# Attention kernel for 32 images: one lane's softmax rows normalised before the turn, its values product taken on two tiles at once

## What is computed

```
# layer 0
h    = group_norm(x) * gn_w + gn_b                     # 32 groups of 4 channels
q,k,v = split(qkv_w @ h + qkv_b)                        # 128 channels each
attn = softmax(q^T k * C**-0.5)                         # 1024 x 1024 per image
x    = x + proj_w @ (v @ attn^T) + proj_b
# layer 1
q,k  = Wq @ x + bq, Wk @ x + bk                         # 16 channels each
v    = Wv @ x + bv                                      # 128 channels
attn = softmax(q^T k)
out  = gamma * (v @ attn^T) + x
```

## Time and profile before

| | |
|---|---|
| median of 3 runs | 1571.02 us (1569.89 to 1573.38) |
| the profiled execution | 1575.76 us |
| its span, first to last instruction | 1573.7 us |
| transposing DMAs | 512, two in a slot |
| slots with tiles | 257 |

### The profile page before, as it was taken

How to read it: one execution, slowest core, us unless ns; L and a number is a source line. 1 busy time by engine, 2 the same in 40 slices (tenths; PEclk the granted TensorE clock), 3 DMA queues, 4 the chain that set the end, 5 groups by cost and what they waited for, 6 DMA issues and landing times.

```text
span 1573.7 us, 43918 instructions
## 1 busy us (share of the span) xinstructions
PE 1482.2 (94%) x16777; PEld 1116.9 (71%) x16777; DVE 1285.6 (82%) x2508; ACT 1218.2 (77%) x1698; POOL 1240.4 (79%) x1027
## 2 busy tenths in 40 slices
PE   4899999999999999999899999999999999999977
PEld 2577777776777777777677777677777777777766
DVE  5678888888888888888788888888888878888885
ACT  3578878887877887878788887887878878888774
POOL 3788888888878887878788888788788878888653
PEclk9899999999999999999999999999999999999999
DMA  3799999999999999999999999999999999999999
GB/s 76 135 161 199 203 197 204 198 206 204 198 195 194 207 203 203 202 193 209 189 202 211 202 194 202 196 202 203 195 199 210 203 190 204 203 193 199 192 200 181
DMA packets 1081437, 305.21 MB, mean 194 GB/s; under 512 B 1068272, under 2 KB 1068944, under 8 KB 1081232
## 3 DMA queue, kind: packets, MB, share of 16 engines
q1 hardware_dynamic: 1066688, 270.42, 105.4%
q10 hardware_dynamic: 14544, 31.99, 6.0%
HBM read 17.13 MB, written 16.78 MB: 22 GB/s over the span
## 4 chain that ended last, share of the span: by engine, by line
SPq 66%; PE 17%; issue 5%; DVE 4%; DMA 3%; ACT 2%; POOL 1%; DVEq 0%; POOLq 0%; ACTq 0%
SPq L299 66%; DMA pt<-rows 3%; PE mixed L823 3%; PE mixed L825 3%; PE mixed L824 3%; PE scores L778 2%; DVE nmax L572 2%; PE scores L779 1%; PE scores L780 1%; DVE rows L589 1%; PE scores L808 1%; PE bank_w L889 1%; PE bank_w L897 1%; ACT scores L457 1%; POOL rows L358 1%
## 5 line engine op out<-in xcount | busy, mean ns | idle before, releaser
L823 PE MATMUL mixed<-v_head,pt 128*128 128x129 f16 x4096 | 719.5, 222 | 35.7 <-DMA pt<-rows 34.6
L572 DVE TENSOR_REDUCE nmax<-scores 128x1 f32<-128x1024 f32 x512 | 620.5, 1217 | 154.8 <-PE scores L808 141.8
L825 PE MATMUL mixed<-v_head,pt 128*128 128x129 f16 x4096 | 718.7, 220 | 0.0
L824 PE MATMUL mixed<-v_tail,pt 128*128 128x128 f16 x4096 | 718.7, 219 | 0.0
L358 POOL TENSOR_TENSOR rows<-prob,rows 128x1024 f16<-128x1024 f32 x256 | 545.4, 2130 | 21.3
L353 POOL TENSOR_SCALAR rows<-prob 128x1024 f16<-128x1024 f32 x256 | 267.9, 1046 | 233.4 <-ACT prob L452 229.9
L457 ACT ACTIVATE scores<-scores,nmax 128x1024 f32<-128x1024 f32 x256 | 278.7, 1089 | 204.2 <-DVE nmax L572 204.2
L823 PEld LDWEIGHTS mixed<-v_head,pt 128*128 128x128 f16 x4096 | 399.0, 97 | 47.1 <-DMA pt<-rows 45.6
L824 PEld LDWEIGHTS mixed<-v_tail,pt 128*128 128x128 f16 x4096 | 405.7, 99 | 2.3
L825 PEld LDWEIGHTS mixed<-v_head,pt 128*128 128x128 f16 x4096 | 397.0, 97 | 0.0
L589 DVE SCALAR_TENSOR_TENSOR rows<-scores,rows 128x1024 f16<-128x1024 f32 x256 | 313.0, 1222 | 35.6 <-ACT rows L465 35.4
(11 more groups left out here) (110 smaller groups left out, 1852.8 us busy)
## 6 DMA issues: line engine op xcount, KB each, us to landing
out_dram<-y ACTq DMA_DIRECT2D x64, 256.0 KB, 3.8
x_raw<-in_x_dram ACTq DMA_DIRECT2D x29, 512.0 KB, 5.2
pt<-rows SPq DMA_TRANSPOSE x512, 5.4
x_raw<-in_x_dram SPq DMA_DIRECT2D x3, 512.0 KB, 4.4
w_qkv<-in_L_conv_qkv_w_dram SPq DMA_DIRECT2D x3, 64.0 KB, 4.1
b_qk<-in_L_conv_bk_dram SPq DMA_DIRECT2D x8, 0.1 KB, 2.3
b_qk<-in_L_conv_bq_dram SPq DMA_DIRECT2D x8, 0.1 KB, 1.9
w_proj<-in_L_conv_proj_w_dram SPq DMA_DIRECT2D x1, 64.0 KB, 4.8
```

The source lines that it names most:

```text
L572: nc.vector.reduce_max(nmax[l][:, tile.i % TILES:tile.i % TILES + 1], scores[l][:, :], AX.X, negate=True).then_inc(maxed[l], 1)
L823: mm(mixed[l][:, 0:C + 1], head, vh[:, p, m, 0:C + 1], start=(m == 0), stop=False)
L824: mm(mixed[l][:, 0:C], head, vt[:, p, m, :], start=False, stop=False)
L825: done = mm(mixed[l][:, 0:C + 1], tail, vh[:, p, m, 0:C + 1], start=False, stop=(m == TILES - 1))
```

## The change

1. Lane 1's rows are normalised when they are split. `exponent1` also sums the row (`accum_out=row_sum`). A second, 1-column activation scales the sum by 1/4096 (`sum_down`). VectorE inverts it (`invert1`), and head and tail are multiplied with the inverse in place of the constant 4096. `head_row1` now waits for `inverted[1]`.
2. Lane 1's values product is `attend_pair`. It takes two tiles (the even one and the odd one behind it) at once, with v as the stationary operand and 2 x 128 columns of `pt` as the moving one. It runs in the slot of the odd tile + 3, so in every second slot. The result has channels in partitions, so `norm` and `back` are gone for lane 1, and one addition of 256 columns for the pair (`add_pair`) follows in the same slot. Lane 1's ring of `pt` has 6 buffers, since a pair frees two at once.
3. VectorE's order is now: both row maxima, the bias, `invert1`, lane 0's addition, the projection's tail, `tail_row1`, `invert0`, the pair's addition.
4. In the fill, the statistics and the group norm of image 2 stand some slots earlier, and the load of image 2 is issued ahead of 16 small loads.

```diff
-RING = 4
+RING = (4, 6)
...
+KEY_HALVES = (ATTEND, ATTEND)
...
+def pair_at(slot):
+    tile = TILE_AT[1].get(slot)
+    return (LANES[1][tile.i - 1], tile) if tile and tile.i % 2 else None
...
-STATS = Steps(-12, -11, first={1: (-11, -11), 2: (-9, -9)})
-GN = Steps(-10, -9, first={2: (-8, -7)})
+STATS = Steps(-12, -11, first={1: (-11, -11), 2: (-11, -11)})
+GN = Steps(-10, -9)
...
             def exponent1(tile):
                 act.wait_ge(maxed[1], tile.i + 1)
-                nc.scalar.activation(scores[1][:, :], scores[1][:, :], ACT.Exp,
-                                     bias=nmax[1][:, tile.i % TILES:tile.i % TILES + 1],
-                                     scale=1.0).then_inc(exped[1], 1)
+                nc.scalar.activation(scores[1][:, :], scores[1][:, :], ACT.Exp, bias=nmax[1][:, at], scale=1.0,
+                                     accum_out=row_sum[:, at]).then_inc(exped[1], 1)
+                act.wait_ge(exped[1], tile.i + 1)
+                nc.scalar.activation(sum_down[:, at], row_sum[:, at], ACT.Copy,
+                                     scale=1.0 / P_UP).then_inc(summed_down, 1)
...
             def head_row1(tile):
-                act.wait_ge(exped[1], tile.i + 1)
+                act.wait_ge(inverted[1], tile.i + 1)
                 nc.scalar.activation(rows[1][:, tile.i % ROWS, 0, :], scores[1][:, :], ACT.Copy,
-                                     scale=P_UP).then_inc(row_headed[1], 1)
+                                     scale=rinv[1][:, tile.i % TILES:tile.i % TILES + 1]).then_inc(row_headed[1], 1)
...
+            def invert1(tile):
+                dve.wait_ge(summed_down, tile.i + 1)
+                nc.vector.reciprocal(rinv[1][:, at], sum_down[:, at]).then_inc(inverted[1], 1)
...
+            def add_pair(pair):
+                out_free(tile)
+                dve.wait_ge(attended[1], pair[1].i // 2 + 1)
+                nc.vector.scalar_tensor_tensor(out=of_pair(into, pair),
+                                               in0=mixed[1][:, 0:2 * C].rearrange("p (t c) -> p t c", c=C),
+                                               scalar=1.0 / P_UP, in1=of_pair(residual[:, tile.p, :], pair),
+                                               op0=ALU.mult, op1=ALU.add).then_inc(done, 2)
...
+            def attend_pair(pair, half):
+                if half == 0:
+                    for tile in pair:
+                        pe.wait_ge(swung[1][tile.i % RING[1]], swings(tile))
+                    if first.i:
+                        last = LANES[1][first.i - 1]
+                        pe.wait_ge((x1_done, y_done)[last.layer], ADDED[1, last.i])
+                into = mixed[1][:, 0:2 * C].rearrange("p (t n) -> p t n", n=C)
+                for m in range(half * PER_HALF, (half + 1) * PER_HALF):
+                    done = split_product(into, vh[:, p, m, 0:C], vt[:, p, m, :], pt[1][:, r:r + 2, m, :],
+                                         pt[1][:, r:r + 2, TILES + m, :], start=(m == 0), stop=(m == TILES - 1))
...
             def body(slot):
-                here = [lane.get(slot - ATTEND) for lane in TILE_AT]
-                for tile in here:
-                    if tile:
-                        attend(tile)
+                here = TILE_AT[0].get(slot - ATTEND)
+                if here:
+                    attend0(here)
+                for half, offset in enumerate(KEY_HALVES):
+                    if pair := pair_at(slot - offset):
+                        attend_pair(pair, half)
```

More of the change, by code:

```diff
@@ L83, with single_adds, pair_adds, adds_in_order @@
 TILE_AT = [{tile.slot: tile for tile in tiles} for tiles in LANES]
+def pair_at(slot):
+    tile = TILE_AT[1].get(slot)
+    return (LANES[1][tile.i - 1], tile) if tile and tile.i % 2 else None
+def single_adds(slot):
+    return [tile for tile in (TILE_AT[0].get(slot - ADD),) if tile]
+def pair_adds(slot):
+    return [pair for pair in (pair_at(slot - KEY_HALVES[1]),) if pair]
+def adds_in_order():
+    count, added = [0, 0], {}
+    for slot in range(FIRST_SLOT, LAST_SLOT + 1):
+        for tiles in [(tile,) for tile in single_adds(slot)] + pair_adds(slot):
+            count[tiles[0].layer] += len(tiles)
+            added.update({(tile.lane, tile.i): count[tile.layer] for tile in tiles})
+    return added
+ADDED = adds_in_order()
 class Steps:
@@ L271, in swings, with of_pair @@
         def swings(tile):
-            return 16 * (tile.i // RING + 1)
+            return 16 * (tile.i // RING[tile.lane] + 1)
+        def of_pair(image, pair):
+            first, step = pair[0].t, pair[1].t - pair[0].t
+            tiles = image.rearrange("p (t c) -> p t c", c=C)
+            first %= tiles.shape[1]
+            return tiles[:, first:first + step + 1:step, :]
         def qk_bank(im, j):
@@ L530, in body @@
                     qk1_copy(im, h)
-                for lane in range(2):
-                    if tile := TILE_AT[lane].get(slot - ATTEND):
-                        norm(tile)
+                if tile := TILE_AT[0].get(slot - ATTEND):
+                    norm(tile)
                 for im, part in W.at(slot):
@@ L732, in body @@
                     row_max(tile)
+                if tile := TILE_AT[0].get(slot):
+                    row_max(tile)
+                    exp_bias(tile)
+                if tile := TILE_AT[1].get(slot):
+                    invert1(tile)
+                for tile in single_adds(slot):
+                    add_turned(tile)
                 for im, part in W.at(slot - 1):
@@ L739, in body @@
                         v1_tail_out(im, part - V1[0])
[L740 to L744, removed]
-                    dve.wait_ge(turned[tile.lane], tile.i + 1)
-                for tile in added:
-                    (x1_out, y_out)[tile.layer](tile)
                 if tile := TILE_AT[1].get(slot):
                     tail_row1(tile)
-                for lane in TILE_AT:
-                    if tile := lane.get(slot - ATTEND):
-                        invert(tile)
+                if tile := TILE_AT[0].get(slot - ATTEND):
+                    invert0(tile)
+                for pair in pair_adds(slot):
+                    add_pair(pair)
                 for im, h in STATS.at(slot):
@@ L829, in adds_done @@
             def adds_done(slot):
-                for lane in TILE_AT:
-                    if tile := lane.get(slot - ADD):
-                        pe.wait_ge((x1_done, y_done)[tile.layer], tile.n * TILES + tile.t + 1)
+                for tile in single_adds(slot):
+                    pe.wait_ge((x1_done, y_done)[tile.layer], ADDED[0, tile.i])
             def evicted_here(slot):
```

122 lines of the change are left out of this document (63 added, 59 removed).

## The result

The changed kernel takes **1790.08 us** (4 runs, 1787.31 to 1795.71) against 1570.64 before: 1.140 times as long, 95% interval 1.136 to 1.143. The forecast was 1690, with a range of 1630 to 1745. The sign and the pattern were right, the size was not: +219 where +119 was forecast.

What follows compares the result with a forecast made beforehand. SyncE's transposes were taken as the bound, 47.3 us an image, TensorE nearly level. Odd slots 27.2 plus even 24.0 made 51.2: +117 us over 30 images, +2 behind them, fill 0, giving 1690 us, range 1630 to 1745.

Steps and rivals of the forecast that it cites:

- The bound before: SyncE's transposing DMAs, queued without gaps, set the old kernel's pace at 47.3 us an image; TensorE's work was 45.1.
- The alternation: Odd slots last as long as TensorE's work, 6.4 to 7.4 us; even ones as long as the chain, 5.8 to 6.2.
- The chain: Lane 1's loop from `score1` through exponent, head and tail to the next `score1`: from 5.30 to 5.80 us.
- the added 0.2 for `h_head`: Slot 2: ScalarE's late `h_head` of slot 1 holds up the exponent, adding 0.2 us to make 6.0.
- 0.4 was put on the statistics: Slot 6: slot 5's statistics, behind the pair's addition on VectorE, delay the next maximum; 0.4 us added, making 6.2.
- Slot 0: The even slot at an image's start, put at the plain chain's 5.8 us with no excess.
- The clock: In the rival "more": TensorE's clock might fall to 1.2 GHz after idling, passing 1745 us; 10% together with remaining stalls.
- Fill and end: Fill taken as 0 (up to 3.2 us gained against 4 lost); the 8 slots behind the steady part +2 us.
- No change: Rival: the transposes keep the pace at 47.3 us an image, so the time stays 1571 us; 7%.
- faster: Rival: TensorE sets the transposes' pace, its work falls from 45.1 to 43.9 us an image, giving 1532 us; 5%.
- The estimate of 98 ns for 256 columns: TensorE's pair products by the skill's issue gaps: 2.34 us a pair, lowering the estimate to about 1655 us.
- The rule in the Trainium skill, Perfetto Trace Analysis, section What "DMA-bound" means: A solid issuing track means bound by the DMA sequencer; by it the time would be the no-change rival's, 1571 us.

Runs made afterwards that it cites:

- the experiment with the copy: The changed kernel with pair halves in two slots, plus ScalarE's copy of layer 1's queries and keys moved ahead of lane 0's exponent: 1631.95 us, 1.039.
- the extra products: The changed kernel plus unread TensorE products in the idle time ahead of `score1`, 18 in slot 2 and 10 in slot 6: 1720.64 us, 1.093.
- the fill's edits alone: The kernel before with only image 2's earlier statistics and group norm, and its load ahead of 16 small ones: 1565.04 us, 0.9957.
- neither: Both parts of the loss undone: the changed kernel with pair halves in two slots and no normalisation of lane 1's rows: 1557.39 us, 0.991.
- the pair without the normalisation: The changed kernel without lane 1's normalisation (no row sum, one-column activation or inverse; constant 4096 as before), whole pair in one slot: 1691.0 us, 1.074.
- slot 2 was filled: The changed kernel plus 18 unread TensorE products in the idle time of slot 2 alone, none in slot 6: 1735.55 us, 1.105.
- the halves: The changed kernel with the second half of each pair's keys, 12 of 24 products, moved to the slot behind: 1638.86 us, 1.041.

## Why the prediction was wrong, point by point

**The bound before, right.** With both parts of the loss undone, SyncE's queue is full again and the time returns to the old one and slightly below.

**The alternation, right.** Odd slots as long as TensorE's work: forecast 6.4, 7.4, 6.5, 6.9; at full clock 6.49, 7.33, 6.52, 6.79. The pair's 24 products take 0.109 each (0.110 taken). Part of that is luck: the 0.204 for 512 columns was a mean over six products 0.216 apart and two of half height (64*128 in rows 5) that start together. With 0.216 the same line gives 0.110, so the lower bound, 0.106, was too low. Moving half of the products undoes the alternation.

**The chain, right but short.** The forecast was 5.80, the trace shows it in slot 2. VectorE and ScalarE there:

```profile
812.22 1.22 DVE L609 TENSOR_REDUCE nmax<-scores 128x1 f32<-128x1024 f32 x1 [0.47 <-PE scores L862]
813.62 1.22 DVE L609 TENSOR_REDUCE nmax<-scores 128x1 f32<-128x1024 f32 x1 [0.17 <-PE scores L834]
...
814.98 0.16 DVE L626 RECIPROCAL rinv<-sum_down 128x1 f32<-128x1 f32 x1
...
816.39 1.28 DVE L630 SCALAR_TENSOR_TENSOR rows<-scores,rinv,rows 128x1024 f16<-128x1024 f32 x1 [0.46 <-ACT rows L504]
```

```profile
813.52 1.08 ACT L494 ACTIVATE scores<-scores,nmax 128x1024 f32<-128x1024 f32 x1
814.52 0.20 ACT L494 ACTIVATION_READ_ACCUMULATOR scores<-scores,nmax 128x1 f32 x1
814.75 0.20 ACT L497 ACTIVATE sum_down<-row_sum 128x1 f32<-128x1 f32 x1
815.24 1.11 ACT L504 ACTIVATE rows<-scores,rinv 128x1024 f16<-128x1024 f32 x1 [0.29 <-DVE rinv L626]
```

From `score1` at 811.79 the inverse starts at 3.19 (forecast 3.18), the head at 3.45 (3.37), the tail at 4.60 (4.43), and the next `score1` comes at 6.03. The sum with the exponent brings a second instruction of 0.20, which I took at nothing in the forecast's sum; it is still mostly hidden behind lane 0's maximum. Head and tail with a factor for each row take 1.11 and 1.28, where the constant took 1.02 and 1.22. I had them unchanged. This is 0.15 of the 0.23. In slot 2 the added 0.2 for `h_head` then covered it by chance: the exponent started at 813.52, 0.08 behind the end of the row maximum, so `h_head` held it up by no more than that. In slot 4 the other term was right: V1's wait for the tail of QK1 sets 6.08 (6.0 forecast), and it stays 6.00 without the normalisation. Slot 6 is 0.25 longer than slot 2, where 0.4 was put on the statistics; no run tried that term apart.

**Slot 0, wrong by 0.5.** The first tile of an image waits for ScalarE's copy of the queries and keys, which is behind both exponents. The row of `score1` says so: 0.54 idle, ended by ACT L539. I had read only the wait for `row_tailed`. Two of the waits in the code are on that instruction, and I costed one. In slot 0 it is 0.43 us by the experiment with the copy. Over an image that experiment gave back 0.26, or 8 us of the whole.

**The clock, the step that failed.** The forecast named it ("if it fell to 1.2 GHz in such places, each odd slot's start would double in part") and gave it, with the stalls, 10% and no size. It is 2.4 us an image (54.1 against 51.7 with the extra products), 69 us of the 219, and it alone puts the result outside the range. The sum had put it at nothing. Its place could have been read off: a slot with 2.9 us of idle time out of 6 was part of the forecast itself. What I took as evidence against it, a full clock over 1200 us, came from a kernel whose TensorE did not idle for long there except in rare waits for a transpose (4.7 us at most), so it said little of this case. And the answer stood in that trace. Its 3 low clocks in the steady part began at 764.8, 1095.9 and 1287.1 us, each in slot 2, each at or within 1 us of the end of such a wait. These waits are the three longest idle times of TensorE between slots 9 and 248; behind the next, 1.71 us, the clock stayed (TensorE's timeline of the kernel before, three places):

```profile
764.86 0.29 PE L823 MATMUL mixed<-v_head,pt 128*128 128x129 f16 x1 [4.51 <-DMA pt<-rows]
...
1095.86 0.26 PE L823 MATMUL mixed<-v_head,pt 128*128 128x129 f16 x1 [2.20 <-DMA pt<-rows]
...
1286.17 0.23 PE L823 MATMUL mixed<-v_head,pt 128*128 128x129 f16 x1 [3.14 <-DMA pt<-rows]
```

So a low clock had once followed 2.2 us of idle time, and the forecast itself put 2.9 into slot 2 of every image.

**Fill and end, wrong by 12.** The first `score1` of layer 1 came at 98.7 (95.3 before), and from the last full image to the end it took 79.1 us in place of 68.4, at a clock of 0.81:

```profile
1714.54:1793.60 79.06, 55.79 (x475) 42.82 (x474) 43.56 (x77) 39.95 (x63) 28.76 (x19) 0.81 0.81 148
```

I had taken 0 and +2. The end is again the clock in part. Before, the same stretch had a clock of 0.95. With the extra products, which stand in some of these slots too, it took 74.4 at 0.91, so 4.7 of the 10.6 came back with the clock; the rest was not tried apart. In the fill, the edits give 5.5 (with the fill's edits alone) and the longer chain and the pair take 9.

**The account** of the difference of the spans, 219.9 us: steady slots at full clock 51.8 - 47.2 = 4.6 an image, 139; low clock 67 (71 by the extra products); fill 3; end 11. By cause, in us an image from 46.6 with neither: normalisation 2.5, whole pair in one slot 3.0 at full clock (49.7 against those 46.6, which hold 1.6 of waits for transposes and low clock themselves) and 1.3 of clock, and 0.7 only where both are there. The clock's own part is 1.3 with the pair alone and 2.4 with both, which would more than cover that; the longer chain does lengthen the idle time in slot 2.

**The rivals.** No change and faster are out. The estimate of 98 ns for 256 columns, worked out from the figures in the Trainium skill, TensorE: Matmul & The Clock Gate, section Back-to-back issue gap, is not borne out: 109 ns. The rule in the Trainium skill, Perfetto Trace Analysis, section What "DMA-bound" means, named the state before rightly (no gap in SyncE's queue), but not the time after: the changed kernel left that state (319 us of waits in 1200).

## What to carry to other kernels

Halving how often work is done does not help if it doubles the work of one step in a fixed order, while the step between is held by a chain through one buffer: look at the longest and shortest step, not at the mean. Count, for each added instruction, what stands in the loop that a single buffer closes, and cost every wait of the instruction that closes it. And when a forecast leaves TensorE idle for a third of a step, put a price on the clock before anything else. A full clock on average over a busy engine is no evidence against it; look in that trace for the longest idle times and for the clock right behind them.

## What the runs showed of the hardware

- An exponent with a row sum is two instructions on ScalarE: 1.09 us as before, and 0.19 to 0.20 for reading the accumulator.
- The same activation of 128 x 1024 from PSUM takes 1.11 us with a factor for each row and 1.02 with a constant; on VectorE the product and subtraction 1.28 against 1.22. The cause was not tried.
- After 2.76 us of idle time TensorE's clock fell to 1.2 GHz, not at once but 0.3 to 1.5 us into the next work (0.8 in the image shown), and slot 3 took about 9.0 us in place of 7.3. With 2.0 us of that idle time filled, it fell in no image.
- The same idle time did not always end in a low clock. Idle time ahead of `score1`, and images of 30 with a low clock in the slot behind it: 2.76 us, 25; 2.06 us (the pair without the normalisation), 25; 1.95 us (ahead of slot 7), 15, and 10 when slot 2 was filled; 1.61 us (the halves), none. Why some images were spared was not tried.
